# Routing table of a mixture of experts: two scaled one-hot operands become one moving operand of 144 columns

## The chip, the core and the metric

The kernel runs on one core of a Trainium2 chip. The metric is the time of one execution on the device, in microseconds. A core has TensorE (matrix products into PSUM), VectorE, ScalarE, GpSimd and SyncE, which work side by side and wait for each other on semaphores.

## The reference

The input is 4 x 1024 tokens of 256 numbers. A layer norm and a mixture of experts with 8 experts of width 256 are added with weight one half, then causal attention with 16 heads, then the same mixture of experts once more.

```python
x = x + 0.5 * _L0_ffn_ref(_layernorm(x), gate_weight, gate_up_proj, down_proj, similarity_matrix)
x = x + _L0_attn_ref(_layernorm(x), W_dq, W_uq, W_dkv, W_uk, W_uv, W_o)
x = x + 0.5 * _L0_ffn_ref(_layernorm(x), gate_weight, gate_up_proj, down_proj, similarity_matrix)
# in _L0_ffn_ref:
probs = jax.nn.softmax(logits.astype(jnp.float32), axis=-1)
top_w, top_i = jax.lax.top_k(probs, K)            # K = 2 of E = 8
...
rerouted = expert_map[top_i]                      # experts that are nobody's first choice may be replaced
...
out = jnp.einsum('ne,enh->nh', combine, y)        # only the chosen experts have weight
```

## The kernel before

The program runs these phases one after the other: for layer a `phase_logits`, `phase_route` and `phase_experts`; then `phase_qkv` and `phase_attention`; then the three phases again for layer b; then `phase_sum`. The tags in the names of the trace say which it is: `ar` and `br` are the two routings, `ae` and `be` the two expert phases, `t` is attention.

The expert phase doesn't compute all experts for all tokens. It takes the 8192 pairs of token and chosen expert (SLOTC = 64 columns of 128), sorted by expert into MT = 72 tiles of 128 rows, and gathers the rows of a tile from DRAM by an index. `phase_route` makes this index. After the choice and the counting, every pair has a place, which is split into a tile (0 to 71) and a lane (0 to 127). The table has to say, for each tile and lane, which pair stands there. It is a sum of products: for one column of 128 pairs, the stationary operand `lane_hot` has a one where a pair's lane is, and the moving operand is a one-hot of the pair's tile, scaled by a number of the pair. A pair's number has two parts, the number of its column (from GpSimd, `tile_col`, L530) and that of its partition (from ScalarE, `tile_lane`, L421). Before, each part has a product of its own into the same 72 columns of PSUM, `ps_table`, where they add up.

The 64 columns are done in 8 rounds of CW = 8 columns. `table_steps` calls a body for rounds 0 and 1 and then for three turns of a loop with two rounds each. In all one-hot tensors the 8 columns of a round are the innermost axis, so the operand of one column is read with a step of 8 elements of float16. A round goes like this:

- VectorE, `hot`: waits until `hot_used` says that the products of round r - 2 are done (two buffers, b = 0 and 1), writes `tile_hot` (L506) and `lane_hot` (L508).
- GpSimd, `by_column` (L530), and ScalarE, `by_lane` (L421): wait for `tile_hot`, write the two scaled tensors.
- TensorE, `add` (L554): waits for `lane_hot` and both scaled tensors, runs 16 products, each with a load of its stationary operand, and signals `hot_used`.

One product with a tile of zeros opens the accumulation (L546) and one closes it (L557) and signals `table_done`. Beside the last rounds VectorE computes each tile's expert (L515 to L517). Then it waits for `table_done`, and three instructions, each of which waits for the one before (`c.link`), make the slots and tokens: `empty` marks the rows that nobody uses (L520), `R.slot` is the number less one (L521), `R.token` its low bits (L522). The expert phase begins with GpSimd's copy of four columns of `R.token` (L606), from which it gathers rows (L619); TensorE transposes them (L656) and multiplies them by the gate and up weights (L670).

The order of the work is the order of the code on each engine; there is no planner.

Of the kernel before, what the change touches and what calls it, by code (L numbers as in the profile page):

```python
# [25 lines left out]
F16 = mybir.dt.float16  # L26
I32 = mybir.dt.int32
ALU = mybir.AluOpType
# [3 lines left out]
P = 128  # L32
# [11 lines left out]
MT = TOPK * N // P + E  # L44
# [65 lines left out]
def bc(ap, axis, shape):  # L110
    return ap.unsqueeze(axis).to_broadcast(shape)
# [247 lines left out]
def phase_route(nc, T, tag, logits, R, W):  # L359


    with ExitStack() as ctx:
        M = Mem(nc, ctx, tag)
# [12 lines left out]
        big = M.sb("big", [P, SLOTC, E])  # L376
        upto = M.sb("upto", [P, SLOTC + 1, E])
        ones = M.sb("ones", [P, SLOTC])
        zeros = M.sb("zeros", [P, MT], F16)
        counts_i, tiles_i = M.sb("counts_i", [P, E], I32), M.sb("tiles_i", [P, E], I32)  # L380
        tiles, tiles_end, row0 = (M.sb(n, [P, E]) for n in ("tiles", "tiles_end", "row0"))
        place, place_i = M.sb("place", [P, SLOTC]), M.sb("place_i", [P, SLOTC], I32)
# [4 lines left out]
        CW = 8  # L387

        number16 = M.sb("number16", [P, P, CW], F16)
        lane_hot = M.sb("lane_hot", [P, 2, P, CW], F16)  # L390
        tile_hot, tile_col, tile_lane = (M.sb(n, [P, 2, MT, CW], F16) for n in ("tile_hot", "tile_col", "tile_lane"))
        empty = M.sb("empty", [P, MT])
        ps_count, ps_before, ps_total, ps_table = (M.ps(n, [P, 512]) for n in ("ps_count", "ps_before", "ps_total", "ps_table"))
        chain_sem, gap_ready, exp_ready, picked_ready, counted, routed_ready, ranked, hot_ready, col_ready, \
            number_ready, hot_used, table_done = (
                M.sem(n) for n in ("chain", "gap_ready", "exp_ready", "picked_ready", "counted", "routed_ready", "ranked",
                                   "hot_ready", "col_ready", "number_ready", "hot_used", "table_done"))
# [3 lines left out]
        def table_steps(eng, body):  # L401

            for b in range(2):
                body(b, b)
            with eng.Fori(1, SLOTC // CW // 2) as it:
                for b in range(2):
                    body(it * 2 + b, b)

        @block.scalar
        def _(act):  # L410
            for e in range(E - W.ROUTED, E):
                W.high(act, e, e % 2)
            act.wait_ge(gap_ready, 1)
            nc.scalar.activation(expgap[:], gap[:], ACT.Exp).then_inc(exp_ready, 1)

            nc.scalar.copy(number16[:], bc(T.iota[:], 2, [P, P, CW])).then_inc(exp_ready, 1)

            def by_lane(r, b):
                act.wait_ge(hot_ready, r * 2 + 1)
                wait(act, hot_used, r - 1)  # L420
                nc.scalar.activation(tile_lane[:, b], tile_hot[:, b], ACT.Copy, scale=T.lane_number[:]).then_inc(number_ready, 1)  # L421
            table_steps(act, by_lane)

        @block.vector
        def _(dve):
            c = Chain(dve, chain_sem)
            v = nc.vector
# [5 lines left out]
            for k in range(TOPK):  # L433
# [4 lines left out]
                ins = v.tensor_tensor(picked[:, k], bc(iota_e, 1, shape), bc(choice[k][:], 2, shape), ALU.is_equal)  # L438
# [39 lines left out]
            for e in range(E):  # L478
                ins = v.tensor_tensor_scan(upto[:, 1:, e], ones[:], total[:, :, e], 0.0, ALU.mult, ALU.add)
# [36 lines left out]
            c.link(v.tensor_reduce(expert_f[:], ended[:], AX_X, ALU.add))  # L516
            c.link(v.tensor_scalar(R.expert[:], expert_f[0:1, :], float(E - 1), None, ALU.min))  # L517
            dve.wait_ge(table_done, 1)
            found = ps_table[:, 0:MT]
            c.link(v.scalar_tensor_tensor(empty[:], found, 0.0, T.unused_row[:], ALU.is_equal, ALU.mult))  # L520
            c.link(v.scalar_tensor_tensor(R.slot[:], found, -1.0, empty[:], ALU.add, ALU.add))  # L521
            c.link(v.tensor_scalar(R.token[:], R.slot[:], N - 1, None, ALU.bitwise_and))  # L522

        @block.gpsimd
# [11 lines left out]
        @block.tensor  # L536
        def _(pe):
            pe.wait_ge(picked_ready, 1)
            nc.tensor.matmul(ps_count[:, 0:NT * E], T.ones_f[:], picked[:, 0].rearrange("p n e -> p (n e)"),
                             start=True, stop=True).then_inc(counted, 1)  # L540
            pe.wait_ge(routed_ready, 1)
            rhs = routed[:].rearrange("p c e -> p (c e)")
            nc.tensor.matmul(ps_before[:], T.lower_bf[:], rhs, start=True, stop=True)
            nc.tensor.matmul(ps_total[:], T.ones_bf[:], rhs, start=True, stop=True).then_inc(ranked, 1)
            pe.wait_ge(hot_ready, 2)
            nc.tensor.matmul(ps_table[:, 0:MT], lane_hot[:, 0, :, 0], zeros[:], start=True, stop=False)  # L546

            def add(r, b):
                pe.wait_ge(hot_ready, r * 2 + 2)
                pe.wait_ge(col_ready, r + 1)  # L550
                pe.wait_ge(number_ready, r + 1)
                for j in range(CW):
                    for number in (tile_col, tile_lane):
                        ins = nc.tensor.matmul(ps_table[:, 0:MT], lane_hot[:, b, :, j], number[:, b, :, j], start=False, stop=False)  # L554
                ins.then_inc(hot_used, 1)
            table_steps(pe, add)
            nc.tensor.matmul(ps_table[:, 0:MT], lane_hot[:, 1, :, 0], zeros[:], start=False, stop=True).then_inc(table_done, 1)  # L557


def phase_experts(nc, T, tag, R, W, xn_dram, y_dram):  # L560
# [982 lines left out]
def program(nc, x, W_dq, W_uq, W_dkv, W_uk, W_uv, W_o, gate, gate_up, down, similarity, out):  # L1543
    with ExitStack() as ctx:
# [42 lines left out]
        def moe(tag, o_rows, *loads):  # L1587
            with ExitStack() as layer:
                W = Weights(nc, T, Mem(nc, layer, tag), gate_up, down)
                phase_logits(nc, T, tag + "l", xs, xn_dram, logits, W, o_rows, *loads)  # L1590
                phase_route(nc, T, tag + "r", logits, R, W)
                phase_experts(nc, T, tag + "e", R, W, xn_dram, y_dram)
# [32 lines left out]
```

## Time and profile before

| | |
|---|---|
| three runs | 1371.19, 1375.2, 1381.31 us, median 1375.2 |
| span of the profiled execution | 1440.9 us |
| instructions in it | 28115 |
| TensorE busy, weight loads, VectorE, ScalarE, GpSimd | 77%, 47%, 59%, 47%, 32% of the span |
| granted TensorE clock, mean | 0.879 of 2.4 GHz |
| DMA | 141.06 MB, mean 98 GB/s |
| table stage of routing a, of routing b | about 84 to 106 us, about 1122 to 1144 us |

The span goes from the first to the last instruction of one profiled execution, which took longer than the three runs shown; no other time of that execution is given. Rows of the timeline have the start in us, the duration in us, the engine (PE is a product, PEld a load of the stationary operand, DVE VectorE, ACT ScalarE, POOL GpSimd), the line of the code, the operation, the tile written and the tiles read with their shape and type, and in brackets how long the engine had been idle before and what released it. A granted clock of 0.50 is 1.2 GHz, and 1.00 is 2.4 GHz. Ends of products are modelled; their starts are the safer number.

### The profile page before, as it was taken

What the parts mean: (1) busy time and instruction counts of PE and PEld (TensorE: products, weight loads), DVE (VectorE), ACT (ScalarE), POOL (GpSimd) and SP (SyncE); (2) the same over time, 40 slices, a digit from 0 to 9 for tenths busy, and PEclk for the clock granted to TensorE, in tenths of its full rate; (3) what the DMA queues carried; (4) which work ended last, traced back from release to release, by engine and by line L of the source; (5) the groups of instructions that cost most, each with busy time, mean ns of one, the idle gap of its engine ahead of it and who ended that gap; (6) DMA issues with size and microseconds to landing.
All of it is one profiled execution on the core that took longest, in us unless ns stands there. A gap on an engine that the chain in (4) does not pass through costs nothing. (4 is left out here: it accounts for less than half of the span.)

```text
span 1440.9 us, 28115 instructions
## 1 busy us (share of the span) xinstructions
PE 1111.1 (77%) x7114; PEld 671.0 (47%) x7117; DVE 853.0 (59%) x2530; ACT 674.2 (47%) x1676; POOL 463.3 (32%) x520
## 2 busy tenths in 40 slices
PE   3458988875786589999899899998694698897840
PEld 2246766664332134444334334443372577676630
DVE  5763333332884688888788788884177533333335
ACT  3513343332455056766666666666454243333320
POOL 3636666653234400000000000000165456665620
PEclk8558999998778589999999999999897599999975
DMA  7502222223586914555544444440273022222238
GB/s 244 182 1 81 82 79 80 83 77 103 179 262 173 167 16 61 78 74 78 73 60 60 61 60 61 72 57 9 84 232 110 19 75 84 80 81 75 76 122 264
DMA packets 130285, 141.06 MB, mean 98 GB/s; under 512 B 46800, under 2 KB 104592, under 8 KB 130192
## 3 DMA queue, kind: packets, MB, share of 16 engines
q1 hardware_dynamic: 116368, 102.24, 31.8%
q0 software_dynamic: 13824, 37.77, 8.3%
q8 instruction: 35, 0.57, 0.2%
q14 instruction: 58, 0.48, 0.1%
HBM read 86.88 MB, written 52.69 MB: 97 GB/s over the span
## 5 line engine op out<-in xcount | busy, mean ns | idle before, releaser
L1407 ACT ACTIVATE t_prob<-t_psS 128x512 f32<-128x512 f32 (+3 forms) x768 | 328.1, 494 | 189.1 <-PE t_psS L1339 155.6
L1427 DVE CUSTOM_DVE_ANT_0 t_psR<-t_psR,all_causal 128x128 f32<-128x128 f32 (+3 forms) x512 | 246.4, 505 | 60.4 <-PE t_psR L1317 52.9
L1317 PE MATMUL t_psR<-stacks_kst,stacks_qst 96*128 96x512 bf16 (+3 forms) x768 | 231.2, 345 | 29.3 <-PEq L886 20.3
L1336 PE MATMUL t_psS<-stacks_qst,stacks_kst 99*128 99x512 bf16 (+3 forms) x768 | 224.0, 329 | 2.7 <-ACT t_prob L1407 2.0
L1431 DVE TENSOR_REDUCE t_maxp<-t_psR 128x1 f32<-128x512 f32 x256 | 176.0, 688 | 21.1 <-PE t_psR L1317 20.3
L1350 PE MATMUL t_psO<-t_prob,t_vst 128*32 128x512 f32 (+3 forms) x1536 | 163.6, 498 | 3.0 <-ACT t_prob L1407 1.1
L1317 PEld LDWEIGHTS t_psR<-stacks_kst,stacks_qst 96*128 96x128 bf16 x768 | 70.1, 98 | 201.0 <-DVE t_maxp L1427 103.1
L1308 POOL COPY t_vst<-stacks_v_rows 128x512 f32<-128x512 f32 x16 | 9.9, 616 | 443.3 <-DMA stacks_v_rows<-v_rows 443.2
L670 PE MATMUL be_psG<-b_w,be_xT 128*128 x432 | 119.8, 413 | 13.0 <-issue 8.6
L670 PE MATMUL ae_psG<-a_w,ae_xT 128*128 x432 | 118.2, 408 | 14.3 <-issue 8.1
L763 DVE TENSOR_TENSOR ae_hid<-ae_sg,ae_psG 128x256 f32<-128x256 f32 x72 | 30.4, 422 | 139.1 <-ACT ae_sg L733 106.8
L763 DVE TENSOR_TENSOR be_hid<-be_sg,be_psG 128x256 f32<-128x256 f32 x72 | 30.3, 422 | 137.6 <-ACT be_sg L733 116.6
L1339 PE MATMUL t_psS<-all_causal_t,all_ident_bf 128*128 128x128 bf16 x512 | 110.1, 220 | 0.0
L1336 PEld LDWEIGHTS t_psS<-stacks_qst,stacks_kst 99*128 99x128 bf16 x768 | 73.7, 98 | 50.1 <-ACT t_prob L1407 26.3
L670 PEld LDWEIGHTS be_psG<-b_w,be_xT 128*128 128x128 f32 x432 | 78.9, 196 | 30.9 <-issue 17.7
L670 PEld LDWEIGHTS ae_psG<-a_w,ae_xT 128*128 128x128 f32 x432 | 77.6, 193 | 32.0 <-issue 19.0
L619 POOL DMA_INDIRECT be_xg<-xn_rows,be_index x72 | 70.5, 979 | 51.0 <-PE be_psX L656 17.8
L619 POOL DMA_INDIRECT ae_xg<-xn_rows,ae_index x72 | 70.6, 981 | 47.5 <-PE ae_psX L656 19.2
L626 POOL DMA_INDIRECT y_rows<-ae_y,ae_target x72 | 71.0, 986 | 41.0 <-issue 18.6
L626 POOL DMA_INDIRECT y_rows<-be_y,be_target x72 | 71.0, 986 | 39.9 <-issue 20.3
L670 PE MATMUL be_psY<-b_w,be_hT 128*128 x432 | 70.5, 299 | 3.4 <-DVE be_hT L756 1.9
L1427 DVE DVE_READ_ACCUMULATOR2_ANT t_maxp<- 128x1 f32 x512 | 72.2, 141 | 0.0
(284 smaller groups left out, 1901.1 us busy)
## 6 DMA issues: line engine op xcount, KB each, us to landing
qk_parts<-q_parts SPq DMA_DIRECT2D x32, 384.0 KB, 2.8
stacks_qst<-qk_parts SPq DMA_DIRECT2D x96, 128.0 KB, 4.7
stacks_kst<-qk_parts SPq DMA_DIRECT2D x96, 128.0 KB, 7.4
q_yk<-y_rows SPq DMA_DIRECT2D x16, 512.0 KB, 5.4
s_yk<-y_rows SPq DMA_DIRECT2D x16, 512.0 KB, 5.4
o_rows<-t_orow SPq DMA_DIRECT2D x32, 136.0 KB, 8.8
bl_raw<-o_rows SPq DMA_DIRECT2D x8, 544.0 KB, 4.0
xn_rows<-al_xn SPq DMA_DIRECT2D x8, 512.0 KB, 4.3
```

Source lines behind the costliest of these rows:

```text
L619: nc.gpsimd.indirect_dma_start(xg[:, i, :], None, xn_dram, bass.IndirectOffsetOnAxis(ap=index[:, s:s + 1], axis=0)).then_inc(x_loaded[i], 16)
L626: nc.gpsimd.indirect_dma_start(y_dram, bass.IndirectOffsetOnAxis(ap=target[:, s:s + 1], axis=0), y[:, i, :], None).then_inc(y_stored[i], 16)
L670: ins = nc.tensor.matmul(out, lhsT[a][:, s % 2, c, :], W.parts[b][:, c, bass.ds(e, 1), cols].rearrange("p a f -> p (a f)"), start=(n == 0) ...
L763: nc.vector.tensor_tensor(hid[:, s % 2, :], sg[:, s % 2, :], psG[s % 2][:, F:2 * F], ALU.mult).then_inc(hid_ready, 1)
L1308: nc.gpsimd.tensor_copy(heads(vst[k], VW)[:, :, 0:DK], heads(v_rows[k], DK)).then_inc(pool_done, 1)
L1317: nc.tensor.matmul(psR[bank][:, 0:w], qst[slot][0:KROWS, h, i * P:(i + 1) * P], kst[slot][0:KROWS, h, k0:k0 + w], start=True, stop=True).t ...
L1336: ins = nc.tensor.matmul(ps, kst[k][0:MROWS, h, j * P:(j + 1) * P], qst[k][0:MROWS, h, a:(c + 1) * 512], start=True, stop=a > j * P)
L1339: ins = nc.tensor.matmul(ps[:, 0:P], T.ident_bf[:], T.causal_t[:], start=False, stop=True)
L1350: ins = nc.tensor.matmul(psO[c][h * VW:(h + 1) * VW, a - c * 512:512], vst[k][:, j, h * VW:(h + 1) * VW], prob[j % 2][:, h, a:(c + 1) * 51 ...
L1407: nc.scalar.activation(prob[j % 2][:, h, a:(c + 1) * 512], psS[n % ST_BANKS][:, a - c * 512:512], ACT.Exp, scale=DK ** -0.5).then_inc(exp_ ...
L1427: ins = nc.vector.tensor_tensor_reduce(psR[bank][:, 0:w], psR[bank][:, 0:w], T.causal[:, 512 - w:512], 1.0, -BIG, ALU.add, ALU.max, maxp[: ...
L1431: ins = nc.vector.tensor_reduce(maxp[:, h, col:col + 1], psR[bank][:, 0:w], AX_X, ALU.max)
```

## The change

The two scaled tensors become two halves of one tile, `numbers`, so that the operand of one column is 144 elements with one step of 8: first the 72 of `tile_col`, then the 72 of `tile_lane`. One product a column, 8 a round, writes 144 columns of PSUM, the sum of the column numbers in the first 72 and that of the partition numbers in the other 72. The products with zeros are 144 columns wide too. What PSUM added up before is now added by VectorE: a copy of the first half out of PSUM, and a sum with the second half, ahead of the three instructions that were there.

```diff
-        zeros = M.sb("zeros", [P, MT], F16)
+        zeros = M.sb("zeros", [P, 2 * MT], F16)
...
-        tile_hot, tile_col, tile_lane = (M.sb(n, [P, 2, MT, CW], F16) for n in ("tile_hot", "tile_col", "tile_lane"))
-        empty = M.sb("empty", [P, MT])
+        tile_hot = M.sb("tile_hot", [P, 2, MT, CW], F16)
+        numbers = M.sb("numbers", [P, 2, 2, MT, CW], F16)
+        tile_col, tile_lane = numbers[:, :, 0], numbers[:, :, 1]
+        empty, column_part, found = (M.sb(n, [P, MT]) for n in ("empty", "column_part", "found"))
...
             dve.wait_ge(table_done, 1)
-            found = ps_table[:, 0:MT]
-            c.link(v.scalar_tensor_tensor(empty[:], found, 0.0, T.unused_row[:], ALU.is_equal, ALU.mult))
-            c.link(v.scalar_tensor_tensor(R.slot[:], found, -1.0, empty[:], ALU.add, ALU.add))
+            c.link(v.tensor_copy(column_part[:], ps_table[:, 0:MT]))
+            c.link(v.tensor_tensor(found[:], column_part[:], ps_table[:, MT:2 * MT], ALU.add))
+            c.link(v.scalar_tensor_tensor(empty[:], found[:], 0.0, T.unused_row[:], ALU.is_equal, ALU.mult))
+            c.link(v.scalar_tensor_tensor(R.slot[:], found[:], -1.0, empty[:], ALU.add, ALU.add))
             c.link(v.tensor_scalar(R.token[:], R.slot[:], N - 1, None, ALU.bitwise_and))
...
-            nc.tensor.matmul(ps_table[:, 0:MT], lane_hot[:, 0, :, 0], zeros[:], start=True, stop=False)
+            nc.tensor.matmul(ps_table[:, 0:2 * MT], lane_hot[:, 0, :, 0], zeros[:], start=True, stop=False)
...
                 for j in range(CW):
-                    for number in (tile_col, tile_lane):
-                        ins = nc.tensor.matmul(ps_table[:, 0:MT], lane_hot[:, b, :, j], number[:, b, :, j], start=False, stop=False)
+                    ins = nc.tensor.matmul(ps_table[:, 0:2 * MT], lane_hot[:, b, :, j],
+                                           numbers[:, b, :, :, j].rearrange("p k t -> p (k t)"), start=False, stop=False)
                 ins.then_inc(hot_used, 1)
             table_steps(pe, add)
-            nc.tensor.matmul(ps_table[:, 0:MT], lane_hot[:, 1, :, 0], zeros[:], start=False, stop=True).then_inc(table_done, 1)
+            nc.tensor.matmul(ps_table[:, 0:2 * MT], lane_hot[:, 1, :, 0], zeros[:], start=False, stop=True).then_inc(table_done, 1)
```

## Rows read from the trace of the kernel before

**Rows 1.** The page's head.

```profile
span 1440.9 us, 28115 instructions
```

**Rows 2.** Instructions on the table tile of routing a; ns minimum/median/maximum.

```profile
L554 PE MATMUL ar_ps_table<-ar_tile_col,ar_lane_hot x64: 308/317/340, 85.9 to 105.0; 128*128 128x72 f16 x64
```

**Rows 3.** Windows: length, busy PE, PEld, DVE, ACT, POOL; PEclk is granted clock.

```profile
85.80:105.30 19.50, 18.06 (x129) 17.15 (x129) 10.31 (x17) 5.44 (x7) 9.81 (x8) 0.50 0.01 2
...
114.00:116.00 2.00, 2.00 (x8) 1.51 (x6) 0.00 (x0) 0.47 (x2) 0.98 (x2) 0.50 0.25 72
116.00:118.00 2.00, 2.00 (x13) 1.70 (x12) 0.84 (x2) 0.89 (x4) 0.95 (x1) 0.94 0.23 59
...
512.00:513.00 1.00, 1.00 (x5) 0.51 (x4) 1.00 (x4) 0.07 (x1) 0.00 (x0) 0.50 0.00 0
```

**Rows 4.** Timeline of VectorE and GpSimd, first rounds and last of both routings.

```profile
83.64 0.46 DVE L506 TENSOR_TENSOR ar_tile_hot<-ar_number,ar_tile 128x576 f16<-128x576 f16 x1
84.18 1.66 POOL L530 TENSOR_TENSOR ar_tile_col<-ar_tile_hot,all_col_number 128x576 f16<-128x576 f16 x1 [15.07 <-DVE ar_tile_hot L506]
84.62 1.54 DVE L506 TENSOR_TENSOR ar_tile_hot<-ar_number,ar_tile 128x576 f16<-128x576 f16 x1
88.47 0.46 DVE L506 TENSOR_TENSOR ar_tile_hot<-ar_number,ar_tile 128x576 f16<-128x576 f16 x1 [1.72 <-PE ar_ps_table L554]
...
100.70 0.46 DVE L506 TENSOR_TENSOR ar_tile_hot<-ar_number,ar_tile 128x576 f16<-128x576 f16 x1 [1.09 <-PE ar_ps_table L554]
...
1121.76 0.46 DVE L506 TENSOR_TENSOR br_tile_hot<-br_number,br_tile 128x576 f16<-128x576 f16 x1
...
1138.38 0.46 DVE L506 TENSOR_TENSOR br_tile_hot<-br_number,br_tile 128x576 f16<-128x576 f16 x1 [1.11 <-PE br_ps_table L554]
```

**Rows 5.** Timeline of TensorE in round 0 of routing a.

```profile
85.91 0.14 PEld L554 LDWEIGHTS ar_ps_table<-ar_tile_col,ar_lane_hot 128*128 128x128 f16 x1 [1.01 <-issue]
85.94 0.31 PE L554 MATMUL ar_ps_table<-ar_tile_col,ar_lane_hot 128*128 128x72 f16 x1 [0.90 <-POOL ar_tile_col L530]
85.95 0.17 PEld L554 LDWEIGHTS ar_ps_table<-ar_tile_lane,ar_lane_hot 128*128 128x128 f16 x1
86.07 0.32 PE L554 MATMUL ar_ps_table<-ar_tile_lane,ar_lane_hot 128*128 128x72 f16 x1
...
88.00 0.32 PE L554 MATMUL ar_ps_table<-ar_tile_lane,ar_lane_hot 128*128 128x72 f16 x1
```

**Rows 6.** Timeline of TensorE, operands with adjacent columns, routing and attention.

```profile
75.91 0.10 PEld L543 LDWEIGHTS ar_ps_before<-ar_routed,all_lower_bf 128*128 128x128 bf16 x1 [11.80 <-DVE ar_routed L467]
...
512.58 0.31 PE L1339 MATMUL t_psS<-all_causal_t,all_ident_bf 128*128 128x128 bf16 x1
512.59 0.15 PEld L1317 LDWEIGHTS t_psR<-stacks_kst,stacks_qst 96*128 96x128 bf16 x1 [0.28 <-issue]
512.69 0.31 PE L1317 MATMUL t_psR<-stacks_kst,stacks_qst 96*128 96x128 bf16 x1
```

**Rows 7.** Timeline of the products with zeros and of routing a's end.

```profile
84.75 0.15 PEld L546 LDWEIGHTS ar_ps_table<-ar_zeros,ar_lane_hot 128*128 128x128 f16 x1 [8.71 <-DVE ar_lane_hot L508]
...
104.35 0.19 DVE L517 TENSOR_SCALAR all_expert<-ar_expert_f 1x72 int32<-1x72 f32 x1
105.24 0.24 PE L557 MATMUL ar_ps_table<-ar_zeros,ar_lane_hot 128*128 128x72 f16 x1
105.58 0.23 DVE L520 SCALAR_TENSOR_TENSOR ar_empty<-ar_ps_table,all_unused_row 128x72 f32<-128x72 f32 x1 [1.04 <-PE ar_ps_table L557]
...
106.12 0.20 DVE L522 TENSOR_SCALAR all_token<-all_slot 128x72 int32<-128x72 int32 x1
106.85 0.19 POOL L606 COPY ae_index<-all_token 128x4 int32<-128x4 int32 x1 [3.93 <-SPq L565]
```

**Rows 8.** Timeline of gate and up products, early and later in expert phase a.

```profile
112.88 2.92 PE L670 MATMUL ae_psG<-a_w,ae_xT 128*128 x6 [0.28 <-issue]
...
120.49 1.56 PE L670 MATMUL ae_psG<-a_w,ae_xT 128*128 x6
```

## The prediction

> **What bounds the kernel now.** I read the page first: one core, span 1440.9 us [rows 1]. The edit touches one stage that runs twice, the building of the row table in the routing of layers a and b. The view that groups instructions by tile shows 64 products of the column numbers in each routing, and the code has as many of the lane numbers, all 72 columns wide, 0.317 us each [rows 2]. In the stretch of the first table, 19.5 us long, TensorE is busy 18.06 us and its granted clock is 0.50, that is 1.2 GHz [rows 3]. A busy TensorE proves little here, so the question is which wait ends last, and the timeline tells it.
>
> The stage is a ring of two buffers: VectorE writes tile_hot(r) and lane_hot(r) once the products of round r-2 are done, GpSimd scales tile_hot(r), then TensorE runs the 16 products of round r. For the first two rounds there is nothing to wait for, and tile_hot ends at 84.10 and at 86.16, 2.06 apart: GpSimd works until 85.84 and holds VectorE's second instruction, which takes 1.54 instead of 0.46 and ends 0.32 after it [rows 4]. From round 2 on VectorE waits for TensorE (1.72 us before 88.47, 1.09 before 100.70), and the seven intervals from the end of tile_hot(0) to that of tile_hot(7) take 101.16 - 84.10 = 17.06 us in a and 1138.84 - 1122.22 = 16.62 in b, where 7 x 2.06 = 14.42 would do. So TensorE's time for a round sets the pace, with 2.64 and 2.20 us to be had at most before VectorE and GpSimd take over.
>
> **What a product costs.** In a round the products start at 85.94, 86.07 and so on to the sixteenth at 88.00 [rows 5]: 2.06 / 15 = 0.137 us from start to start, each with a weight load of its own. The whole forecast hangs on what this 0.137 is made of, since the change halves the pairs of load and product and doubles the columns of each.
> - Is it the pair? In attention, at the same clock of 0.50 [rows 3], products of 128 adjacent columns, each with its own load of 128 columns, start 0.11 apart (512.58, 512.69) [rows 6]. So a pair with 56 more columns is quicker than ours. Loads take 0.15 there and 0.14 to 0.15 here. Only a load that starts alone is longer here, 0.15 against 0.10 [rows 6, 7]: its elements lie 16 bytes apart (CW = 8 elements of 2 bytes). But the loads at 85.91 and 85.95 end 0.07 apart (86.05 and 86.12), and the second product still starts 0.13 after the first [rows 5]. Loads could come at twice the pace of the products.
> - Is it the moving columns? They lie 16 bytes apart too. The closing product with zeros has 72 adjacent columns and the same kind of load, and takes 0.24 [rows 7] where its neighbours take 0.317 [rows 2]. These 0.08 us are what lies between 0.137 and the 0.06 that 72 columns take at 1.2 GHz. So I read the 0.137 as 72 strided columns at 1.9 ns each.
>
> The Trainium skill, "SBUF — State Buffer", in its note on SBUF cachelines, says that a 16-byte line has to be hit at least twice for full bandwidth, and that each access to a new line pays. The change keeps one hit per line. By that rule, as by the row, the price goes with the columns, and the trace agrees (0.24 against 0.317).
>
> **The change, step by step**, for one routing:
> 1. Products in a round: 16 of 72 become 8 of 144. A trace of before has no strided product of another width, so I bound it. Below: the pair sets the pace, 0.137 each. Above: every column at 1.9 ns, 0.274. In between: the 72 new columns at the pace of adjacent ones, 0.137 + 0.06 = 0.197. I take 0.274, because the three comparisons above speak for columns. A round is then 8 x 0.274 = 2.19 us as 16 x 0.137 = 2.19 was. VectorE's release came 0.47 after the start of the last product (88.00 to 88.47 [rows 4, 5]) and now comes 0.14 later than that, while the last of 8 starts 7 x 0.274 = 1.92 after the first, not 2.06. So the release stands where it stood. Sum for the loop: 0 us.
> 2. The 64 weight loads that go: 0, since they lie under the products.
> 3. The two products with zeros are 144 adjacent columns instead of 72: + 0.06 each. The opening one runs before TensorE's wait of 0.90 for GpSimd, which ends at 85.94 [rows 5], so its part is hidden; if that wait were gone it would cost its 0.06. The closing one is on the path: + 0.06.
> 4. VectorE's tail. After the closing product VectorE ran three dependent instructions, L520 to L522, starting at 105.58 and 106.12 for the first and third, so 0.27 a link, and GpSimd's first index copy waits for them at 106.85 [rows 7]. Now two come ahead: a copy of 72 elements out of PSUM and a sum of it with the other 72. Both read PSUM as L520 and L521 do: 0.27 each. In exchange the two that follow read SBUF; L522, which reads SBUF, takes 0.20 where L520 takes 0.23, so each may be 0.03 shorter. So + 0.48 to + 0.54, I take 0.50. Nothing hides it: the whole core waits for this chain, and behind it stand the token index, GpSimd's gathers and the experts' first product.
> 5. The memset of the zeros tile at the head of the phase gets 72 more elements; a whole VectorE instruction on 72 takes 0.20 [rows 7], so it is between 0 and some 0.1, and I take 0. Writing both scaled tensors into one tile changes no instruction on ScalarE or GpSimd, and no wait or DMA is added or moved.
>
> Sum: 0 + 0.06 + 0.50 = 0.56 a routing, 1.1 us for two. Against the profiled execution: 1440.9 + 1.1 = 1442.0. The median of the runs shown, 1375.2, is 65.7 us (4.6%) under that span, and the stage is a fixed pattern, so I put the same 1.1 us on it: 1376.3.
>
> **Rival 1, the pair sets the pace (faster).** If a pair costs 0.137 whatever its columns, or 0.197, a round takes 1.1 or 1.6 us. The point at which it decides: products of round r-1 start 0.10 after GpSimd (85.84 to 85.94), that is 0.22 before tile_hot(r) ends, and their release has to come before GpSimd ends round r, 1.74 after (84.10 to 85.84). That gives 7 steps plus 0.53 below 1.96, so a step below 0.204. Under it the loop runs at 2.06 a round and gives back 2.64 and 2.20 us. At the tail the closing product comes 1.10 earlier (0.62 at 0.197), of which VectorE can use some 0.95, since it is busy until 104.54 with the expert numbers and starts L520 at 105.58 [rows 7]. With 0.56 for steps 3 and 4: 2.64 + 0.95 - 0.56 = 3.0 in a and 2.20 + 0.95 - 0.56 = 2.6 in b, 5.6 us in all, 1369.6; at 0.197 it is 2.7 and 2.3, 1370.2. For it: the longer load that starts alone. Against it: the three comparisons. Chance 0.15.
>
> In a sentence apart: the Trainium skill, "TensorE: Matmul & The Clock Gate", section Back-to-back issue gap, gives N / 1.2 ns between products on the cold clock, 60 for 72 columns and 120 for 144; with its load time of 128 / 1.2 = 107 ns a pair would go from 107 to 120, an estimate by which this rival holds; the trace has 137 where the page has 107.
>
> **Rival 2, the clock rises later in the experts (slower).** The place is the start of the experts' phase: the clock is still 0.50 at 114 to 116 and 0.94 at 116 to 118 [rows 3], and six products of gate and up take 2.92 us at the lower level against 1.56 at the higher [rows 8]. If the phase stayed on the lower clock longer, each further microsecond would cost about half a microsecond: 1 - 1.56 / 2.92 = 0.47. Five more in each layer: 4.7, with the 1.1 above 1381.0. It beats the best of rival 1 from 12 us more, and 1% is reached at some 27 us. Against it: TensorE streams as many columns as before at the same pace, it was at 0.50 through the whole table stage though busy 18.06 of 19.50 us, and 7 us lie between its last product and the first of gate and up anyway [rows 7, 8]. Chance 0.05.
>
> That the change does not do what it says, with the 144 columns issued as two operands, is hardly possible: both halves have one stride, and a tile's 72 x 8 elements follow on each other. If it were so, the tail's 1.1 us would remain.
>
> **How the numbers follow.** Forecast (the columns set the pace, + 1.1) 0.80, rival 1 0.15, rival 2 0.05. Predicted time 1376.3. The runs shown spread from 1371.2 to 1381.3, so a median may lie 4 to 6 us off even if nothing changes. The range goes from rival 1 with 3 of that, 1366, to the forecast with 6, 1382. A measurement of this kernel tells about 1%, 13.8 us, from no change, and no case has that: faster 0.02, same 0.95, slower 0.03, the last from rival 2's far end.
>
> **What would show it.** In the profile after: 64 products of 144 columns a routing in place of 128 of 72, starting 0.27 apart (step 1; 0.14 to 0.20 for rival 1) and some 0.45 long; tile_hot from the first to the last in about 17 us (14.4 for rival 1), with VectorE still waiting for TensorE; five links after the closing product instead of three, 1.0 us from the first start to the last instead of 0.54 (step 4); loads still 0.15. It is wrong if the starts come less than 0.20 apart, or if VectorE no longer waits for TensorE in the loop.

## The result: 1% slower, and the profile after

The changed kernel takes 1389.9 us (median of 4 runs, 1388.3 to 1391.4) against 1376.0 us of the kernel before on the same chip (4 runs, 1371.2 to 1381.3). The ratio is 1.0098, with a 95% interval from 1.0072 to 1.0125: 14 us slower where 1.1 was forecast, and outside the range.

The stage that was edited looks much as forecast. Here are the page's head, TensorE's row on the table tile (ns minimum/median/maximum, first and last start), and from the timeline VectorE's first and last tile_hot, a round's eight products merged into one row, the tail and GpSimd's first index copy.

```profile
span 1388.6 us, 27865 instructions
```
```profile
L556 PE MATMUL ar_ps_table<-ar_numbers,ar_lane_hot x64: 428/442/461, 88.0 to 106.4; 128*128 128x144 f16 x64
```
```profile
85.66 0.46 DVE L508 TENSOR_TENSOR ar_tile_hot<-ar_number,ar_tile 128x576 f16<-128x576 f16 x1
...
87.96 2.25 PE L556 MATMUL ar_ps_table<-ar_numbers,ar_lane_hot 128*128 128x144 f16 x8 [0.84 <-POOL ar_numbers L533]
...
102.30 0.46 DVE L508 TENSOR_TENSOR ar_tile_hot<-ar_number,ar_tile 128x576 f16<-128x576 f16 x1 [1.04 <-PE ar_ps_table L556]
...
107.11 0.23 DVE L521 COPY ar_column_part<-ar_ps_table 128x72 f32<-128x72 f32 x1 [0.98 <-PE ar_ps_table L560]
...
108.18 0.20 DVE L525 TENSOR_SCALAR all_token<-all_slot 128x72 int32<-128x72 int32 x1
...
108.90 0.18 POOL L609 COPY ae_index<-all_token 128x4 int32<-128x4 int32 x1 [4.39 <-SPq L568]
```

Against [rows 2]: 64 products of 144 columns in 0.442 us each in place of 128 of 72 in 0.317. Eight take 2.25 us with the last one's 0.44, so they start 1.81 / 7 = 0.259 apart, 1.80 ns a column. VectorE still waits for TensorE at the last round (1.04 where [rows 4] have 1.09). From the first tile_hot to the index copy it is 108.90 - 85.66 = 23.24 us; before it was 106.85 - 83.64 = 23.21 [rows 4, 7]. The 14 us are not in this stage.

Where they are, the page's lines on the instruction queues and TensorE's waits give away. Here are two lines of the page after: packets and MB of two queues that carry the engines' own code.

```profile
q8 instruction: 53, 0.87, 0.3%
q14 instruction: 59, 0.48, 0.1%
```

The same two lines of the profile of before:

```profile
q8 instruction: 35, 0.57, 0.2%
q14 instruction: 58, 0.48, 0.1%
```

So 18 packets came on q8, though the changed program is the shorter one. A packet of q8 has 0.87 MB / 53 = 16.4 KB. In attention, in the timeline after, TensorE stands still twice in each of two turns of the loop with no releaser but "issue": the profile shows nothing that it waits for.

```profile
674.91 0.61 PE L1320 MATMUL t_psR<-stacks_kst,stacks_qst 96*128 96x512 bf16 x1 [3.60 <-issue]
679.10 0.61 PE L1339 MATMUL t_psS<-stacks_qst,stacks_kst 99*128 99x512 bf16 x1 [2.20 <-issue]
...
780.19 0.60 PE L1320 MATMUL t_psR<-stacks_kst,stacks_qst 96*128 96x512 bf16 x1 [3.42 <-issue]
784.37 0.61 PE L1339 MATMUL t_psS<-stacks_qst,stacks_kst 99*128 99x512 bf16 x1 [2.19 <-issue]
```

### The profile page after: what moved, and what is told of

Same layout as the page of the kernel before. It is cut to its first block and busy times, and to the rows that moved or that the text cites. A ratio compares the mean times of both kernels' runs of the same rounds, so it can differ in the third digit from the quotient of the medians.

```text
span 1388.6 us, 27865 instructions
## 1 busy us (share of the span) xinstructions
PE 1095.8 (79%) x6988; PEld 650.9 (47%) x6989; DVE 855.4 (62%) x2534; ACT 679.2 (49%) x1676; POOL 461.9 (33%) x520
## 5 line engine op out<-in xcount | busy, mean ns | idle before, releaser
L1410 ACT ACTIVATE t_prob<-t_psS 128x512 f32<-128x512 f32 (+3 forms) x768 | 329.0, 495 | 205.2 <-PE t_psS L1342 172.1
L1339 PE MATMUL t_psS<-stacks_qst,stacks_kst 99*128 99x512 bf16 (+3 forms) x768 | 229.2, 337 | 6.6 <-issue 4.4
L673 PE MATMUL be_psG<-b_w,be_xT 128*128 x432 | 115.7, 404 | 9.5 <-DVE be_xT L755 6.0
L673 PE MATMUL ae_psG<-a_w,ae_xT 128*128 x432 | 114.6, 401 | 9.7 <-DVE ae_xT L755 6.1
L622 POOL DMA_INDIRECT be_xg<-xn_rows,be_index x72 | 70.3, 976 | 32.8 <-issue 12.8
L736 ACT ACTIVATE be_sg<-be_psG 128x256 f32<-128x256 f32 x72 | 27.6, 383 | 85.4 <-PE be_psG L673 85.4
```

The source lines that it names most:

```text
L622: nc.gpsimd.indirect_dma_start(xg[:, i, :], None, xn_dram, bass.IndirectOffsetOnAxis(ap=index[:, s:s + 1], axis=0)).then_inc(x_loaded[i], 16)
L673: ins = nc.tensor.matmul(out, lhsT[a][:, s % 2, c, :], W.parts[b][:, c, bass.ds(e, 1), cols].rearrange("p a f -> p (a f)"), start=(n == 0) ...
L736: nc.scalar.activation(sg[:, s % 2, :], psG[s % 2][:, 0:F], ACT.Silu).then_inc(sg_ready, 1)
L1339: ins = nc.tensor.matmul(ps, kst[k][0:MROWS, h, j * P:(j + 1) * P], qst[k][0:MROWS, h, a:(c + 1) * 512], start=True, stop=a > j * P)
L1410: nc.scalar.activation(prob[j % 2][:, h, a:(c + 1) * 512], psS[n % ST_BANKS][:, a - c * 512:512], ACT.Exp, scale=DK ** -0.5).then_inc(exp_ ...
```

## The experiments

**The theory.** TensorE's code comes from DRAM in blocks of 16 KB, through q8. Attention's loop is the one large loop of the kernel: three groups of heads written out, 1426 TensorE instructions in the kernel's instruction list (a product counts as two, its load and itself; registers and the branch are in it), run three times. That count is too low, as the table of moved code will show: some 1717 is nearer. The change takes 4 x 8 pairs, 64 instructions, out of routing a's code (two rounds written out and two in the loop), and with that all code behind it moves forward. If the loop then lies over one block more than the core keeps, its code is fetched anew in each turn. **The rivals:** the change itself costs the time (clock, DMA, less regular work), or VectorE's two new instructions move VectorE's code.

All experiments but those on strides move code or undo one part. The padding products are 8 columns wide, ones by ones, their results are overwritten, and they run while TensorE waits for other engines: 64 of them took 1.90 us of an idle time of 11.

### The kernel before, once more

A second profile of the kernel before was needed, since the expert phases of the first take 33 to 35 us longer each than those after, and its attention is 16 us shorter.

> The kernel before, unchanged in what it computes and in its instructions. The profile shown of before has a span of 1440.9 us where its runs take 1375, and its expert phases are 33 us longer each than those of the changed kernel, its attention 16 us shorter. Both theories expect a time near 1376 us here. If the span is near 1376 too, its phases can be set against those of the changed kernel: the theory of code position expects attention (first to last t_psO product) near 506 us against 522, 35 instruction packets on queue 8, none or few in the third turn of attention's loop, and expert phases equal to within 2 us. The rival, that the extra time is spread (DMA, clock), expects attention within 5 us of 522 and the 14 us elsewhere.

It took 1375.1 us, with a span of 1373.4. From the first to the last product of t_psO attention takes 990.3 - 481.1 = 509.2 us, and 1004.2 - 482.2 = 522.0 in the changed kernel. The last y_rows of experts a are issued at 314.2 and 313.8, and the stage of routing a takes 23.22 us here (109.03 - 85.81). So 13 us, nearly the whole difference, are in attention. Between marks three groups apart (the product of t_maxq), the turns of the loop give this; the fences hold the rows of q8 and q14 in the DMA view for before's second turn (629.11 to 730.91), for after's second turn (632.04 to 737.51) and for after's third (737.51 to 843.06).

```profile
q14 instruction: 12, 0.10, 0.4%
q8 instruction: 3, 0.05, 0.3%
```
```profile
q8 instruction: 9, 0.15, 0.6%
q14 instruction: 12, 0.10, 0.4%
```
```profile
q8 instruction: 9, 0.15, 0.6%
q14 instruction: 11, 0.09, 0.3%
```

| | turn 1 | turn 2 | turn 3 | next 3 groups |
|---|---|---|---|---|
| before: us, packets on q8 | 95.3, 6 | 101.8, 3 | 99.9, none | 94.7, 4 |
| after: us, packets on q8 | 96.8, 6 | 105.5, 9 | 105.5, 9 | 94.9, 6 |

Before, the third turn fetches nothing, so all blocks that the loop lies over are on the core; after, turns 2 and 3 fetch nine each. The other queue is alike in both.

### The changed kernel with the code back in its place

```diff
+            for _ in range(32 if tag == "ar" else 0):
+                nc.tensor.matmul(ps_table[:, 0:8], T.ones_bf[:], T.ones_bf[:, 0:8], start=True, stop=True)
             pe.wait_ge(routed_ready, 1)
```

> The changed kernel with 32 more products (8 columns, ones by ones, results overwritten) on TensorE in routing a, while it waits for the routed tensor, so that all of TensorE's code behind it stands 64 instructions later, where it stood before the change. Theory of code position (attention's loop is 1426 TensorE instructions, its code is fetched in blocks of 16 KB, and after the change it lies over one block more than stays on the core): 1376 to 1378 us, attention near 506 us, about 35 instruction packets on queue 8, no idle time of 2 us or more put down to issue in the loop. Rival (the change itself costs it: clock, DMA, VectorE's code): 1390 us as the changed kernel, attention 522 us.

1376.8 us (10 runs), ratio 1.0020 (0.9996 to 1.0044). TensorE does more work than in the changed kernel, and the kernel is 12 us faster, each set against the kernel before on its own chip (+ 13.9 and + 1.7). The waits of its third turn (733.39 to 831.93), engine and what it waited for, us in total, times, longest:

```profile
PEld t_psO L1355 <- issue: 4.1, 15, 0.4
PEld t_psR L1322 <- issue: 2.3, 5, 0.8
PE t_psR L1322 <- issue: 0.2, 1, 0.2
```

The same view of the changed kernel's third turn (737.51 to 843.06):

```profile
PEld t_psR L1320 <- issue: 7.2, 11, 3.7
PEld t_psO L1353 <- issue: 4.5, 15, 0.8
PE t_psR L1320 <- issue: 3.4, 1, 3.4
PEld t_psS L1339 <- issue: 2.8, 2, 2.6
PE t_psS L1339 <- issue: 2.2, 1, 2.2
```

With the code back in place, no wait of TensorE for issue is longer than 0.8 us; q8 has 35 packets in all, 3 in turn 2 and none in turn 3, which takes 98.5 us.

### The same padding behind attention

The same two lines with `tag == "br"`: the same instructions, but behind attention in the code.

> The changed kernel with the 32 padding products in routing b instead of a, so behind attention in the code: the same number of instructions as the padded kernel that took 1376.8 us. Theory of code position: attention's loop stands where it stood in the changed kernel, 1389 us, attention 515 to 522 us. Rival (the padding products help by their number, or by work given to TensorE): 1377 us.

1391.3 us (5 runs), ratio 1.0099 (1.0068 to 1.0129); 53 packets on q8, nine in each of turns 2 and 3, attention 522.8 us. So it is neither the number of padding products nor the work that they give TensorE. It is where the loop stands.

### The kernel before with its code moved

The padding alone, in routing a of the kernel before: 64, 128 and 20 products, which move the code by 128, 256 and 40 instructions.

> The kernel before with 64 such products added in routing a at the same place, nothing else changed: TensorE's code behind stands 128 instructions (half a block) later. Theory of code position: the loop again lies over one block more, about 1390 us, attention near 522 us, about 53 instruction packets on queue 8. Rival: nothing that takes time is added outside a wait of 11 us, so 1376 us.

> The kernel before with 128 padding products in routing a instead of 64: TensorE's code behind moves by 256 instructions, one whole block of 16 KB. Theory of code position (what counts is where the loop stands within a block, not how much code there is): 1375 to 1377 us again, attention near 507 us, no waits of 2 us for issue in its loop, 36 instruction packets on queue 8. Rival (more code in front costs more, whatever the position): 1390 us or above.

> The kernel before with 20 padding products in routing a: TensorE's code behind moves by 40 instructions. Six blocks of 256 hold 1536 instructions and the loop has some 1426, so it fits into six over a window of some 110 starting places and needs seven elsewhere. The starts 64 earlier and 128 later were bad, so the window begins at most 64 before the present start and ends at least 46 behind it: 40 has to be good by this theory. 1376 to 1378 us, 35 or 36 instruction packets on queue 8, 3 and 0 of them in the second and third turn of the loop. Rival (the time rises steadily with the shift): about 4 us more than before, 1380 us.

| start of the loop against before, instructions | us | ratio, 95% | q8 packets in the profile; turns 2, 3 | attention in the profile, us |
|---|---|---|---|---|
| - 64 (the changed kernel) | 1389.9 | 1.0098 (1.0072 to 1.0125) | 53; 9, 9 | 522.0 |
| 0 (before) | 1375.1 | | 35; 3, 0 | 509.2 |
| + 40 (20 products) | 1381.3 | 1.0042 (1.0017 to 1.0068) | 53; 9, 9 | 517.0 |
| + 128 (64 products) | 1387.1 | 1.0106 (1.0055 to 1.0156) | 54; 9, 9 | 514.9 |
| + 256 (128 products) | 1377.9 | 1.0003 (0.9979 to 1.0026) | 36; 3, 0 | 509.6 |

Each ratio is against the kernel before on the same chip, whose medians lie from 1375.1 to 1377.5. Nothing of the computation is touched in the last three, and a half block of padding costs by its runs what the change cost, while a whole block costs nothing. This fits a period of 256 instructions, which with 16.4 KB a packet makes 64 bytes each.

The row of + 40 went against my expectation, and the traces show why: the loop is longer than 1426. The instruction list has each product of t_psO once, 48 in a group of heads and so 768 in 16 groups; the trace has 1536, since each of these float32 products is there as two. The window of before's second turn shows 699 products and as many loads:

```profile
L1350 PE MATMUL t_psO<-t_prob,t_vst x1536: 272/551/1062, 481.1 to 990.3; 128*32 128x512 f32 x96, 128*32 128x384 f32 x32, 128*32 128x256 f32 x32, 128*32 128x128 f32 x32
```
```profile
629.11:730.91 101.80, 95.04 (x699) 39.75 (x699) 82.82 (x267) 64.69 (x150) 1.85 (x3) 0.97 0.46 64
```

With the list's 319 other entries for the loop (registers, waits, the branch) that is an estimate of 1717, 6.7 blocks. The whole of TensorE's code, counted so, is 9092 instructions or 35.5 blocks, and the profile has 35 packets. Such a loop lies over seven blocks from only some 75 of 256 starts and over eight from the others. So 0 can be good with - 64 and + 40 both bad, and by this count seven blocks are kept where eight are not. That the nine packets of a bad turn are these eight and one more ahead is likely and not shown.

Nine packets don't have one price. In the profiles of + 128 and + 40 TensorE has a single long wait a turn; here is one of each:

```profile
674.31 0.61 PE L1319 MATMUL t_psR<-stacks_kst,stacks_qst 96*128 96x512 bf16 x1 [4.11 <-issue]
...
683.43 0.39 PE L1319 MATMUL t_psR<-stacks_kst,stacks_qst 96*128 96x512 bf16 x1 [4.21 <-issue]
```

Their attention takes 5.7 and 7.8 us more than before's, not 12.8. Why the place sets the price is open. So is the spread of + 40, whose ten runs lie from 1377.9 to 1391.8 where those of + 256 lie from 1372.3 to 1381.7. Its profile is of a run at 1390.8, and 6 us of what that has over before lie between the experts and attention (the last y_rows of experts a to the first product of t_maxq takes 162.2 us, before 156.2), where the kernel with adjacent operands below, whose code isn't moved, has 162.9. No quick run of + 40 was profiled, so whether it fetches in every run isn't shown.

Of the Trainium skill, "Runtime: NRT & Kernel Launch", section Instruction fetch mechanics: code comes in 16 KiB blocks of 256 instructions, TensorE's memory for it holds 128 KiB, and a taken branch to code that is not held is a stall. The trace agrees with the blocks and the stalls (16.4 KB a packet, good places 256 apart, waits of 2.2 to 4.3 us). The page also calls it two blocks in all; here a turn of a loop of 6.7 blocks fetched none, so on TensorE it is more.

### VectorE's part alone

```diff
-                    for number in (tile_col, tile_lane):
-                        ins = nc.tensor.matmul(ps_table[:, 0:MT], lane_hot[:, b, :, j], number[:, b, :, j], start=False, stop=False)
+                    for k, number in enumerate((tile_col, tile_lane)):
+                        ins = nc.tensor.matmul(ps_table[:, k * MT:(k + 1) * MT], lane_hot[:, b, :, j], number[:, b, :, j],
+                                               start=False, stop=False)
```

and the copy and sum of the change.

> The kernel before with only VectorE's part of the change: the products stay 72 wide and 16 a round, but the column numbers go to the first 72 columns of PSUM and the partition numbers to the next 72, and VectorE copies and adds them (two instructions more in each routing). TensorE's code stays where it was. Theory of code position: + 0.5 us a routing from the longer tail, 1377 us, attention near 506 us. Rival (VectorE's two instructions more move VectorE's code, and that costs the 14 us): 1390 us.

1377.1 us (10 runs), ratio 1.0020 (0.9989 to 1.0051), 35 packets on q8, attention 509.6 us. VectorE's code moves by as much as in the changed kernel and costs nothing that can be told from the tail. That rival falls.

### What a strided column costs

Step 1 was argued from other rows. These two kernels measure it: the scaled tensors are stored column by column, so that the moving elements are adjacent; GpSimd and ScalarE write with a step instead. First in the kernel before, two products of 72:

```diff
-        tile_hot, tile_col, tile_lane = (M.sb(n, [P, 2, MT, CW], F16) for n in ("tile_hot", "tile_col", "tile_lane"))
+        tile_hot = M.sb("tile_hot", [P, 2, MT, CW], F16)
+        tile_col, tile_lane = (M.sb(n, [P, 2, CW, MT], F16) for n in ("tile_col", "tile_lane"))
...
-                nc.gpsimd.tensor_tensor(tile_col[:, b], tile_hot[:, b], ...
+                nc.gpsimd.tensor_tensor(tile_col[:, b].rearrange("p c t -> p t c"), tile_hot[:, b], ...
...
-                        ins = nc.tensor.matmul(..., number[:, b, :, j], ...)
+                        ins = nc.tensor.matmul(..., number[:, b, j, :], ...)
```

> The kernel before with the scaled tensors stored column by column (GpSimd and ScalarE write them with a step), so that the 72 moving elements of a product lie next to each other; all counts and TensorE's code position stay. Theory of step 1 (0.137 us are 72 columns 16 bytes apart): product starts fall from 0.137 to 0.06 to 0.11 us apart, VectorE stops waiting for TensorE in the loop, and the time falls by up to 5 us, if the writes with a step are no slower. Rival (the pair of load and product, or the load with a step, sets the pace): starts stay 0.137 apart, 1375 us.

> The changed kernel with the same storage, one moving operand of 144 adjacent elements, and the 32 padding products in routing a, so that attention's loop stands where it stood before. Theory of step 1: product starts fall from 0.27 to 0.12 us apart, the loop runs at VectorE's and GpSimd's pace, 4 to 5 us less than the padded changed kernel, 1372 us. Rival (strides do not matter): 0.26 apart, 1377 us.

The timeline of TensorE and the rows by tile of the first of them:

```profile
90.12 0.26 PE L555 MATMUL ar_ps_table<-ar_tile_col,ar_lane_hot 128*128 128x72 f16 x1
90.18 0.26 PE L555 MATMUL ar_ps_table<-ar_tile_lane,ar_lane_hot 128*128 128x72 f16 x1
90.24 0.25 PE L555 MATMUL ar_ps_table<-ar_tile_col,ar_lane_hot 128*128 128x72 f16 x1
```
```profile
L531 POOL TENSOR_TENSOR ar_tile_col<-ar_tile_hot,all_col_number x8: 2700/2856/3134, 86.8 to 108.6; 128x576 f16<-128x576 f16 x8
...
L422 ACT ACTIVATE ar_tile_lane<-ar_tile_hot,all_lane_number x8: 2793/2880/2887, 86.8 to 108.3; 128x576 f16<-128x576 f16 x8
```

The products now start 0.06 us apart where [rows 5] have 0.137, with the same loads of lane_hot, still with their step. In the 144-wide kernel eight take 1.15 us with the last one's 0.33, so 0.117 apart where the changed kernel has 0.259. So the pace was the moving columns': 1.8 to 1.9 ns each with a step of 16 bytes, 0.8 when adjacent, and neither the pair nor the load. But the kernels got slower, 1386.9 (ratio 1.0062, 1.0038 to 1.0085) and 1386.2 us (1.0071, 1.0048 to 1.0094), at 35 packets on q8: GpSimd's and ScalarE's writes with a step take 2.8 to 2.9 us each (medians) where they took 1.3 to 1.7 and 0.78. I had put that in as a condition; it decided the time.

### A version with no such step

So the one-hots of the tiles are made column by column from the start: VectorE compares an adjacent row of tile numbers (one more small tile) with each column's number.

```diff
-                v.tensor_tensor(tile_hot[:, b], number16[:, 0:MT], bc(tile[:, cols], 1, tiles_of),
+                v.tensor_tensor(tile_hot[:, b], bc(iota16[:], 1, tiles_of), bc(tile[:, cols], 2, tiles_of),
...
-                nc.gpsimd.tensor_tensor(tile_col[:, b], tile_hot[:, b], bc(T.col_number[:, cols], 1, [P, MT, CW]),
+                nc.gpsimd.tensor_tensor(tile_col[:, b], tile_hot[:, b], bc(T.col_number[:, cols], 2, [P, CW, MT]),
```

> The kernel before with all one-hots of the tiles made column by column from the start (VectorE compares an adjacent row of tile numbers with one broadcast number a column), so that no engine writes or reads with a step of 16 bytes but the loads of lane_hot. Theory of step 1: product starts 0.06 apart as in the kernel with adjacent operands, GpSimd and ScalarE back at 1.3 to 1.7 and 0.8 us, VectorE's tile_hot up from 0.46 to at most 0.7; the loop at 2.1 to 2.3 us a round and the tail 0.9 shorter: 2 to 3 us less than before for both routings, 1373 us. Rival (broadcasting along the innermost axis makes VectorE or GpSimd much slower): 1375 us or above.

> The same storage with the change's one product of 144 adjacent columns, VectorE's two instructions more and the 32 padding products in routing a. Both cost TensorE the same 0.06 us for 72 columns, so by step 1 and step 4 this is the other plus the longer tail, 1.1 us more: 1374 us. Rival (fewer, wider products pay once the columns are adjacent): 1 us less than the other.

With two products of 72: 1372.4 us (12 runs), ratio 0.9966 (0.9948 to 0.9984), faster than the kernel before by 5 us. With one of 144, the longer tail and the padding: 1374.3 us, 0.9983 (0.9963 to 1.0003), 2 us behind it as expected, though the two intervals overlap. The first one's rows of VectorE and GpSimd:

```profile
85.72 0.76 DVE L508 TENSOR_TENSOR ar_tile_hot<-ar_iota,ar_tile 128x576 f16<-128x576 f16 x1
...
96.53 1.47 DVE L508 TENSOR_TENSOR ar_tile_hot<-ar_iota,ar_tile 128x576 f16<-128x576 f16 x1 [0.20 <-PE ar_ps_table L556]
...
105.76 0.23 DVE L522 SCALAR_TENSOR_TENSOR ar_empty<-ar_ps_table,all_unused_row 128x72 f32<-128x72 f32 x1
...
107.02 0.18 POOL L608 COPY ae_index<-all_token 128x4 int32<-128x4 int32 x1 [2.92 <-SPq L567]
```

VectorE waits 0.20 us for TensorE in a round, not 1.1 to 1.7, and its instruction, 0.76 when alone, is now held up by GpSimd's. From the first tile_hot to the index copy it is 21.30 us against 23.21 [rows 4, 7]. At the tail there is no wait at all: VectorE's own expert numbers end last. One column of this profile misleads: it gives a granted clock of 1.00 for this stage, as the second profile of before does, but the products start 0.06 apart here and 0.137 there, as in the profiles with 0.50.

## Why the prediction was wrong

- **What bounds the stage, and step 1 (the columns set the pace).** Right. Forecast 0.274 us a product of 144, measured 0.259, and the adjacent version shows the cause. The loop ends up 0.4 us shorter than before (tile_hot first to last, 102.30 - 85.66 = 16.64 against 17.06 [rows 4]), not 0: a column costs 1.80 ns in the wider product, not 1.90. Rival 1 could only have come with a step below 0.204.
- **Step 2 (the 64 weight loads that go: 0).** This is the step that failed. I priced removed instructions by their time alone, and found them hidden. What they also take away is length: 64 instructions of code in front of attention, and by that their price was 13 us. The sentence "no wait or DMA is added or moved" in step 5 fails with it: 18 packets of 16 KB were added on q8 (35 to 53), and TensorE waits for them. A hint was there before the run in the page's row of q8 (35 packets, 0.57 MB), which the prediction doesn't mention: the code comes in pieces of 16 KB, about as many as the whole code has, so the loop was not fetched anew. How near it was to the size that isn't kept, no row of before shows.
- **Steps 3 and 4 (the tail, + 0.56 a routing).** The mechanism was right: five links, 108.18 - 107.11 = 1.07 from the first start to the last against 0.54 [rows 7], so + 0.53, where 0.50 was forecast. The two that now read SBUF aren't shorter (0.23). With the shorter loop, routing a's stage grows by 0.03 us and routing b's by 0.14 (1127.39 - 1104.58 = 22.81, from 22.67). By these stages the sum of 1.1 us is 0.2; the padded kernel's ratio of 1.0020 (0.9996 to 1.0044) can't tell the two apart.
- **Rival 2 (the clock).** The clock was 0.61 at 116 to 118 us where it was 0.94 [rows 3], but the whole stage stood 2 us later in this execution. From the first index copy to the last y_rows experts a take 313.8 - 108.90 = 204.9 us, and 314.2 - 109.03 = 205.2 in the second profile of before. It played no part.
- **The range.** It was built on what the edit does where it stands, and on the spread of runs. A cause far behind the edit was in no case.

## What to carry to other kernels

A large loop on TensorE can cost time by where its code stands: if an edit changes the number of instructions in front of one, read the packets of the instruction queues and the waits for "issue" in each turn before judging the edit, and pad to the old place to see what the edit itself does. Here 64 instructions fewer cost 14 us, 64 dummy ones brought 12 of them back, and both were larger than anything in the edited stage. And halving a count of products halves nothing when the columns set the pace: adjacent elements did (0.137 to 0.06 us), but only once no other engine had to write with the step.

## What the runs showed of the hardware

- A loop of some 1717 TensorE instructions (an estimate; 6.7 blocks of 256) ran its third turn without one fetch in two places, and with nine in three others. The price was 4 to 7 us a turn, with two waits of 2.2 to 3.6 us, in the changed kernel, and 1.4 to 4.2 us, with one wait of 3.7 to 4.3, in the two others.
- The moving operand with a step of 16 bytes costs 1.8 to 1.9 ns a column at 1.2 GHz, and 0.8 when adjacent. Loads with the same step don't hold up a stream of pairs 0.06 us apart.
- A pair with 8 columns takes (1.90 - 0.17) / 63 = 0.027 us at 1.2 GHz, loads of 128 columns included.
- A write with a step of 144 bytes (float16) makes ScalarE's 128x576 go from 0.78 to 2.88 us and GpSimd's from 1.40 to 2.86. VectorE's compare of that size goes from 0.46 to 0.76 when one operand is broadcast along the innermost axis and the other along the middle one, in place of one along the middle one alone.
